# Graph attention on one core: the one-hots of the source numbers made at another place of the step, against numbers kept in PSUM

## The chip, the cores and the metric

The kernel runs on one core of a Trainium2 chip. The metric is the time of one execution in device microseconds. Five engines run their own instruction queues side by side: TensorE (PE, with its weight loads as PEld), VectorE (DVE), ScalarE (ACT), GpSimd (POOL) and SyncE (SP, which issues DMAs). They meet only through semaphores that one raises and another waits for.

## The reference

A graph has 3125 nodes of 128 features and 53125 edges, sorted by their target node `dst`. Two layers follow each other:

```
h = relu(layernorm(x))
Q, K, V = h @ Wq + bq, h @ Wk + bk, h @ Wv + bv          # 8 heads of 16
scores  = sum(Q[dst] * K[src]) * scale + edge_attr @ We + be
probs   = softmax of scores over the edges of one dst
x = x + segment_sum(probs * V[src], dst) @ Wo + bo
h = relu(layernorm(x));  h = logmap0(h) @ W.T + b
deg = in-degree + out-degree of each node, at least 1
x = x + expmap0(segment_sum(h[src] / sqrt(deg[src] * deg[dst]), dst))
```

The change touches only a side product of the first layer: the out-degrees, which are counts of each node number among the edges' sources `src`.

## The kernel before

A first stage makes Q, K and V for all nodes and writes them to tables in HBM. The attention loop then goes over the edges in 32 groups of 13 x 128 edges (`GROUPS`, `T`, `P`); a group's work on one engine is called its step here, and step g works on group g. Each engine has its own hand-written loop over the groups, whose order is the order of the code; two buffers of almost everything (index `b`) let an engine prepare group g + 1 during step g. The second layer comes after the loop.

What one step does, by engine:

- POOL gathers K and V rows of the next group into `kv` (13 indirect DMAs, line 812). It is held back to certain points of PE's step (`keep_step`).
- PE multiplies the target one-hots `ST` with a window of Q rows (`query`, line 1838, in four chunks of 4, 4, 4 and 1 tiles; chunks 0 and 1 of group g + 1 are done late in step g, chunks 2 and 3 early in step g + 1). Chunks share two PSUM buffers `ps_q`, so chunk 2 may start only when DVE has read chunk 0 out of the first (`s_prod`). PE also spreads row numbers (line 1825) that ACT turns into `ST` (lines 1608, 1610), sums the weighted rows of the group before (`window_sums`, line 1857), turns four small results around (`ps_b`: lines 1845, 1886, 1897, 1900), multiplies the two source one-hots into a histogram of source numbers (line 1892), and runs 16 matmuls whose result nobody reads (`stay_busy`, line 1815).
- DVE multiplies `kv` with `ps_q` (`product`, line 1080) and sums it by head (line 1086), chunk by chunk; adds the bias (line 1099); then four scans give a running maximum over the edges of one target, forward and backward within a partition (lines 1107, 1128) and over partitions (lines 1118, 1139), each with a PE turn between; then it weights the V rows (`weigh`, line 1164), prepares small matrices for the next step (lines 1135, 1026, 1030, 1156), and goes on to `product` of the next group.

The source one-hots: a source number is split into a high part (50 values) and a low part (64 values, `LO`), and `source_one_hots` (line 1050) compares the 13 parts of each partition with all 50 or 64 numbers, giving `oh_hi` (650 bf16 elements per partition) and `oh_lo` (832). The numbers to compare with lie in SBUF as `rep_hi`, in bf16, each number repeated 13 times. DVE's two instructions for group g + 1 stand in step g before and behind the first scan, where the scan waits for DVE's own bias add:

```
V.tensor_tensor(sc[:], sc[:], p_bias..., ALU.add).then_inc(s_sc, 1)
if more:
    source_one_hots(g + 1, 1 - b, (0,))
dve.wait_ge(s_sc, g + 1)
...                                     # the scan, raises s_v1
if more:
    source_one_hots(g + 1, 1 - b, (1,))
```

PE waits for them (`s_oh`) only before the histogram of group g + 1, a step later.

Of the kernel before, what the change touches and what calls it, by code (L numbers as in the profile page):

```python
# [23 lines left out]
ALU = mybir.AluOpType  # L24
# [3 lines left out]
P = 128  # L28
# [4 lines left out]
T = 13  # L33
# [12 lines left out]
HI, LO = 50, 64  # L46
# [98 lines left out]
def build(nc, x, src_t, dst_t, dst_before, dst_after, dst_first, dst_run, src_run, attr, wqkv, bqkv, we, be, wo, bo, w1t, b1,  # L145
# [14 lines left out]
    with ExitStack() as ctx:  # L160
        def sb(name, shape, dt=F32):
            return ctx.enter_context(nc.sbuf_tensor(name, shape, dt))

        def pb(name, shape, dt=F32):
            return ctx.enter_context(nc.psum_tensor(name, shape, dt))

        def sem(name):
            return ctx.enter_context(nc.semaphore(name))
# [3 lines left out]
        iota = sb("iota", [P, P])  # L172
# [42 lines left out]
        rep_hi = sb("rep_hi", [P, LO, T], BF16)  # L215
# [134 lines left out]
        ps_b = pb("ps_b", [P, 512])  # L350
# [7 lines left out]
        p_c2 = ps_b[:, 416:416 + H]  # L358
        p_rc = ps_c[:, 0:C + 1]
        p_fb = ps_c[:, 256:256 + H]  # L360

        s_in = sem("s_in")
        s_w = sem("s_w")
# [34 lines left out]
        s_oh = sem("s_oh")  # L398
# [131 lines left out]
        def known(g):  # L530

            return isinstance(g, int)
# [340 lines left out]
        def _(dve):  # L873
            V = nc.vector
            pre = Steps(nc, dve, s_dv0, 0)
# [10 lines left out]
            def set_idx(g, b, ready):  # L886

                V.tensor_copy(idx[:, b, :], src_i[:, g, :] if known(g) else
                              src_i[:, bass.ds(g, 1), :].rearrange("p g t -> p (g t)")).then_inc(ready, 1)
# [126 lines left out]
            def col(tile, g):  # L1016
                return tile[:, g:g + 1] if known(g) else tile[:, bass.ds(g, 1)]

            def col3(tile, g):
                return (tile[:, g:g + 1, :] if known(g) else tile[:, bass.ds(g, 1), :]).rearrange("p g t -> p (g t)")  # L1020

            def shift_matrix(g, b, used, ready):

                if not (known(g) and g < 2):
                    dve.wait_ge(used, g - 1)
                V.tensor_scalar(shift[:, b, :], imj[:], col(delta, g), None, ALU.is_equal).then_inc(ready, 1)
# [7 lines left out]
            edge_one_hots(0, 0, s_S, TA)  # L1034

            pre.mark(V.tensor_copy(iota_b[:], iota[:]))
            pre.mark(V.tensor_copy(rep_hi[:], iota[:, 0:LO].unsqueeze(2).to_broadcast([P, LO, T])))
            pre.then(V.tensor_scalar(part_i, src_i[:], 6, None, ALU.logical_shift_right))
            pre.then(V.tensor_copy(hi_f[:], part_i))
# [4 lines left out]
            def source_one_hots(g, b, parts=(0, 1)):  # L1044

                if 0 in parts and not (known(g) and g < 2):
                    dve.wait_ge(s_hist, g - 1)
                for i in parts:
                    oh, part, m = ((oh_hi, hi_f, HI), (oh_lo, lo_f, LO))[i]
                    V.tensor_tensor(oh[:, b], col3(part, g).unsqueeze(1).to_broadcast([P, m, T]),  # L1050
                                    rep_hi[:, 0:m, :], ALU.is_equal).then_inc(s_oh, 1)

            def add_counts(g):
                dve.wait_ge(s_hist, g + 1)
# [4 lines left out]
            def flat(tile):  # L1059
                return tile[:].rearrange("p h t -> p (h t)")  # L1060

            def reset8(tile, g):
                return (tile[:, g:g + 1] if known(g) else tile[:, bass.ds(g, 1)]).rearrange("p g h t -> p (g h t)")
# [7 lines left out]
            def scores(g, b, st, more, old):  # L1071

                def product(c):
                    t0, t1 = CH[c]
                    w = t1 - t0
                    dve.wait_ge(s_kv[b][c], 16 * w * ((g - b) // 2 + 1) if known(g) else (g + (2 - b)) * (8 * w))
                    dve.wait_ge(s_qt, NCH * g + c + 1)
                    if c >= 2:
                        st.sync()
                    V.tensor_tensor(prod[:, c % 2, 0:w, :], kv[:, b, t0:t1, 0:D],  # L1080
                                    ps_q[c % 2][:, 0:w * D].rearrange("p (t d) -> p t d", d=D), ALU.mult).then_inc(s_prod, 1)

                def per_head(c):
                    t0, t1 = CH[c]
                    dve.wait_ge(s_prod, NCH * g + c + 1)
                    st.mark(V.tensor_reduce(sc[:, :, t0:t1].rearrange("p h t -> p t h"),  # L1086
                                            prod[:, c % 2, 0:t1 - t0, :].rearrange("p t (h d) -> p t h d", d=DH),
                                            AX_X, ALU.add))

                product(0)  # L1090
                for c in range(NCH):
                    if c == OLD_ROWS:
                        settle(g, b, old)
                    if c + 1 < NCH:
                        product(c + 1)
                    per_head(c)
                st.sync()
                dve.wait_ge(s_bias, g + 1)
                V.tensor_tensor(sc[:], sc[:], p_bias.rearrange("p (t h) -> p h t", h=H), ALU.add).then_inc(s_sc, 1)
                if more:  # L1100
                    source_one_hots(g + 1, 1 - b, (0,))
                dve.wait_ge(s_sc, g + 1)

                if known(g) and g == 0:
                    dve.wait_ge(s_reset8, H)
                    dve.wait_ge(s_line, 16)
                V.tensor_tensor_scan(out=flat(f1), data0=reset8(fwd_reset8, g), data1=flat(sc), initial=BIG,
                                     op0=ALU.add, op1=ALU.max).then_inc(s_v1, 1)
                if more:
                    source_one_hots(g + 1, 1 - b, (1,))  # L1110

            def scan_partitions(g, b, st):

                dve.wait_ge(s_v1T, g + 1)
                if not (known(g) and g < 2):
                    dve.wait_ge(s_cfT, g - 1)
                st.mark(V.tensor_copy(c1[:, b, 0:1], c1[:, 1 - b, P:P + 1]))
                V.tensor_tensor_scan(out=c1[:, b, 1:P + 1], data0=lines(g), data1=p_v1, initial=c1[:, 1 - b, P:P + 1],
                                     op0=ALU.add, op1=ALU.max).then_inc(s_cf, 1)
# [47 lines left out]
            def carry(g, b, st):  # L1167

                dve.wait_ge(s_rc, g + 1)
                st.mark(V.tensor_scalar(fb[:], p_fb, 1.0, None, ALU.add))  # L1170
                st.mark(V.tensor_copy(R[:, b, C:C + 1], p_rc[:, C:C + 1]))
                st.sync()
                st.mark(V.tensor_tensor(R[:, b, 0:C].rearrange("p (h e) -> p h e", h=H),
                                        p_rc[:, 0:C].rearrange("p (h e) -> p h e", h=H),
                                        fb[:].unsqueeze(2).to_broadcast([P, H, DH + 1]), ALU.mult))

            def add_sums(g, b, st):

                st.sync()
                V.tensor_tensor(R[:, b, :], R[:, b, :], ps_r[:, 0:C + 1], ALU.add).then_inc(s_R, 1)  # L1180
# [27 lines left out]
            def settle(g, b, old):  # L1208

                if old:  # L1210
                    new_rows(g - 2, b)
                if not (known(g) and g == 0):
                    add_counts(g - 1)

            def step(g, b, edges=True, nodes=True, more=True, far=True, old=True):

                A = Steps(nc, dve, s_dA, NA * g)
                B = Steps(nc, dve, s_dB, NB * (g - 1))
                if edges:
                    scores(g, b, A, more, old)  # L1220
                else:
                    settle(g, b, old)
                if edges:
                    scan_partitions(g, b, A)
                if nodes:
                    carry(g - 1, 1 - b, B)
                if edges:
                    backward(g, b, A)
                if nodes:
                    add_sums(g - 1, 1 - b, B)  # L1230
                if edges:
                    if far:
                        set_idx(g + 2, b, s_idx)
                    scan_partitions_back(g, b, A)
                    shifted(g, b, A)
                if nodes:
                    average(g - 1, 1 - b, B)
                    B.check(NB)
                if edges:
                    weigh(g, b)  # L1240
                    first_row(g, A)
                    if more:
                        shift_matrix(g + 1, 1 - b, s_rc, s_S)
                        edge_one_hots(g + 1, 1 - b, s_S, TA)
                if edges:
                    factor(g)
                    A.check(NA)

            source_one_hots(0, 0)

            def tile_ids(k, st, idx_ready, rep_ready):
# [855 lines left out]
```

## Time and profile before

| | |
|---|---|
| median of 3 runs | 929.62 us (922.36 to 932.06) |
| profiled execution, its span | 938.0 us |
| PE busy | 824.9 us, 88% |
| DVE busy | 695.7 us, 74% |
| POOL busy | 588.5 us, 63% |
| ACT busy | 537.9 us, 57% |
| attention loop | about 46 to 625 us of the span |

The profile is of another execution than the three timed ones, and gives no time for itself beside its span; that span is 8.4 us above the median of the timed runs. Busy shares are means over the whole program. In a timeline a row is one or several equal instructions in a row: start, duration, engine, line, operation, output<-inputs, how many, and in brackets the idle time of the engine before it and what ended it. Starts of DVE instructions that wait for nothing lie a little before the end of the one ahead, since they overlap. Step 14 ends and step 15 begins at about 334 us; this pair of steps is the one that is read closely.

### The profile page before, as it was taken

Reading aid. Unit: us, or ns where it says so; the run is one execution under the profiler, and the core shown is the slowest. Engines: PE = TensorE matmul, PEld = TensorE weight load, DVE = VectorE, ACT = ScalarE, POOL = GpSimd, SP = SyncE. Lnnn points to the kernel's source line nnn. Section 1 sums busy time; section 2 is a strip of 40 time slices with the busy share of each in tenths; the row PEclk is TensorE's granted clock in tenths of the full one; section 3 lists DMA queues with packets and bytes.
Section 4 is the critical chain, followed back from the end, with each engine's and each line's share of the span. In section 5 each row is a group of like instructions: output and inputs, shape, how many; then the busy total and the mean of one; then the engine's idle time right before and its main releaser. Section 6 shows DMA issues by size and latency. Waiting matters only on the chain.

```text
span 938.0 us, 21433 instructions
## 1 busy us (share of the span) xinstructions
PE 824.9 (88%) x5435; PEld 625.1 (67%) x5435; DVE 695.7 (74%) x2543; ACT 537.9 (57%) x1360; POOL 588.5 (63%) x597
## 2 busy tenths in 40 slices
PE   5559988999999999999999999976599889989983
PEld 3236766767777777777677677764487677868673
DVE  8827745777777776787777777778988878888752
ACT  4486634566666666666665666607765455555530
POOL 0177755667777777777677777700466666666662
PEclk9868977999999999999999999997799999999997
DMA  6653445554544444444444444420422222222221
GB/s 175 208 137 90 115 105 95 113 126 117 128 123 118 136 113 119 131 117 120 128 113 126 128 115 133 120 77 19 107 58 60 65 53 70 56 67 59 64 60 28
DMA packets 103595, 95.99 MB, mean 102 GB/s; under 512 B 35964, under 2 KB 87393, under 8 KB 103553
## 3 DMA queue, kind: packets, MB, share of 16 engines
q0 software_dynamic: 25600, 66.10, 26.2%
q1 hardware_dynamic: 77961, 29.51, 12.7%
q8 instruction: 12, 0.20, 0.1%
q14 instruction: 22, 0.18, 0.1%
HBM read 84.40 MB, written 11.15 MB: 102 GB/s over the span
## 4 chain that ended last, share of the span: by engine, by line
PE 59%; POOL 14%; issue 9%; DMA 7%; DVE 5%; ACT 4%; SPq 2%; POOLq 0%; DVEq 0%
POOL kv L851 14%; PE ps_s L1815 13%; PE ps_q L1838 11%; PE ps_r L1857 10%; PE ps_f L1892 5%; DMA kv<-hs_tab,idx 4%; PE ps_c L1807 4%; PE ps_s L1825 4%; ACT ST L1608 3%; PE ps_f L1916 1%; PE ps_f L1915 1%; PE ps_c L1803 1%; PE ps_r L2017 1%; DMA qwin<-q_tab 1%; PE ps_c L1865 1%
## 5 line engine op out<-in xcount | busy, mean ns | idle before, releaser
L812 POOL DMA_INDIRECT kv<-kv_tab,idx x416 | 418.0, 1005 | 192.3 <-issue 125.3
L851 POOL DMA_INDIRECT kv<-hs_tab,idx x176 | 170.3, 967 | 141.0 <-DMA hs_tab<-qkv 54.4
L1608 ACT ACTIVATE ST<-ps_s,imj 128x512 f32<-128x512 f32 (+1 forms) x128 | 77.1, 602 | 150.1 <-PE ps_s L1825 150.0
L1815 PE MATMUL ps_s<-rep_hi,iota_b 128*128 128x512 bf16 x506 | 139.3, 393 | 0.0
L1838 PE MATMUL ps_q<-qwin,ST 128*128 128x128 f32 x832 | 128.6, 296 | 9.5 <-DMA qwin<-q_tab 6.0
L1838 PEld LDWEIGHTS ps_q<-qwin,ST 128*128 128x128 f32 x832 | 111.2, 201 | 24.8 <-issue 20.5
L1591 ACT ACTIVATE S<-iota,nloc 128x128 f32<-128x128 f32 x384 | 122.0, 389 | 0.0
L1080 DVE TENSOR_TENSOR prod<-kv,ps_q 128x512 f32<-128x512 f32 (+1 forms) x128 | 71.6, 575 | 62.7 <-PE ps_q L1838 60.4
L1857 PE MATMUL ps_r<-wv,S 128*128 128x137 f32 x832 | 111.1, 286 | 0.0
L1857 PEld LDWEIGHTS ps_r<-wv,S 128*128 128x128 f32 x832 | 103.4, 192 | 7.7 <-issue 6.8
L2017 PE MATMUL ps_r<-qkv,xt 128*128 128x128 f32 x800 | 92.0, 276 | 0.8 <-ACT xt L1733 0.8
L2017 PEld LDWEIGHTS ps_r<-qkv,xt 128*128 128x128 f32 x800 | 90.6, 192 | 1.1 <-issue 1.1
L1722 ACT ACTIVATE S<-iota,rest_nloc 128x128 f32<-128x128 f32 x176 | 56.3, 388 | 53.2 <-PE ps_f L2009 53.2
L1610 ACT ACTIVATE ST<-ST 128x512 f32<-128x512 f32 (+1 forms) x128 | 70.3, 550 | 4.0
L1815 PEld LDWEIGHTS ps_s<-rep_hi,iota_b 128*128 128x128 bf16 x506 | 42.3, 99 | 44.2 <-issue 15.4
L2028 PE MATMUL ps_f<-kv,S 128*128 128x128 f32 x352 | 46.9, 294 | 27.6 <-DMA kv<-hs_tab,idx 27.6
L1086 DVE TENSOR_REDUCE sc<-prod 128x32 f32<-128x512 f32 (+1 forms) x128 | 70.9, 574 | 0.0
L1825 PE MATMUL ps_s<-dloc_g,pick 32*128 32x512 bf16 (+1 forms) x128 | 44.9, 350 | 29.5 <-ACT ST L1608 22.4
L1487 DVE TENSOR_SCALAR ST<-bwd_reset 128x800 bf16<-128x800 f16 x128 | 56.3, 440 | 16.8 <-PE ps_q L2000 16.7
L2028 PEld LDWEIGHTS ps_f<-kv,S 128*128 128x128 f32 x352 | 44.4, 207 | 31.2 <-issue 20.4
L1164 DVE TENSOR_TENSOR wv<-kv,wv 128x1024 f32<-128x1024 f32 x64 | 62.5, 1019 | 0.5 <-ACT wv L1626 0.5
L1594 ACT ACTIVATE S<-S 128x512 f32<-128x512 f32 x96 | 60.5, 630 | 3.0
(278 smaller groups left out, 1382.1 us busy)
## 6 DMA issues: line engine op xcount, KB each, us to landing
kv<-kv_tab,idx POOLq DMA_INDIRECT x416, 2.8
attr_s<-in_attr SPq DMA_DIRECT2D x32, 192.0 KB
kv<-hs_tab,idx POOLq DMA_INDIRECT x176
kv_tab<-qkv SPq DMA_DIRECT2D x4, 640.0 KB, 3.4
x_tab<-x SPq DMA_DIRECT2D x32, 64.5 KB, 2.3
qwin<-q_tab SPq DMA_DIRECT2D x32, 64.0 KB
xwin<-in_x SPq DMA_DIRECT2D x32, 64.0 KB
xwin<-x_tab SPq DMA_DIRECT2D x32, 64.0 KB
```

The source lines that it names most:

```text
L812: pool.indirect_dma_start(out=kv[:, b, t, :], out_offset=None, in_=kv_tab, in_offset=bass.IndirectOffsetOnAxis(ap=idx[:, b, t:t + 1], axis ...
L851: pool.indirect_dma_start(out=kv[:, j, t, 0:D], out_offset=None, in_=hs_tab, in_offset=bass.IndirectOffsetOnAxis(ap=idx[:, j, t:t + 1], ax ...
L1080: V.tensor_tensor(prod[:, c % 2, 0:w, :], kv[:, b, t0:t1, 0:D], ps_q[c % 2][:, 0:w * D].rearrange("p (t d) -> p t d", d=D), ALU.mult).then ...
L1086: st.mark(V.tensor_reduce(sc[:, :, t0:t1].rearrange("p h t -> p t h"), prod[:, c % 2, 0:t1 - t0, :].rearrange("p t (h d) -> p t h d", d=DH ...
L1591: A.activation(S[:, b, t, :], iota[:], ACT.Abs, bias=nloc[:, g, t:t + 1] if known(g) else nloc[:, bass.ds(g, 1), t:t + 1].rearrange("p g t ...
L1608: A.activation(ST[:, b, t0:t1, :], row_index(c), ACT.Abs, bias=imj[:, 0:1], scale=-1.0).then_inc(s_sta, 1)
L1815: M.matmul(ps_s[1][:], iota_b[:], busy_cols, start=True, stop=True)
L1825: M.matmul(row_index(c), pick[:, b, :], dloc_g[:, t0:t1, :], start=True, stop=True)\
L1838: mm = M.matmul(ps_q[c % 2][:, (t - t0) * D:(t - t0 + 1) * D], ST[:, b, t, :], qwin[:, b, :], start=True, stop=True)
L1857: mm = M.matmul(ps_r[:, 0:C + 1], S[:, b, t, :], wv[:, t, :], start=(t == 0), stop=(t == T - 1))
L2017: M.matmul(sums[0], counts[:, i, :], hs_t[:, i, :], start=(i == 0), stop=False)
L2028: M.matmul(sums[1], S[:, j, t, :], kv[:, j, t, 0:D], start=(t == 0), stop=False)
```

## The change

Sixty-four fp32 numbers (0 to 63) are copied once into a free part of the PSUM bank `ps_b`. Both one-hot instructions of a group compare with these, each number read 13 times over, in place of `rep_hi`. And both move to the end of DVE's step, behind `weigh` and `first_row`, ahead of the preparation of the shift matrix. `rep_hi` stays, since `stay_busy` reads it.

```
+        p_iota = ps_b[:, 424:424 + LO]
...
+            pre.mark(V.tensor_copy(p_iota, iota[:, 0:LO]))
...
                     V.tensor_tensor(oh[:, b], col3(part, g).unsqueeze(1).to_broadcast([P, m, T]),
-                                    rep_hi[:, 0:m, :], ALU.is_equal).then_inc(s_oh, 1)
+                                    p_iota[:, 0:m].unsqueeze(2).to_broadcast([P, m, T]), ALU.is_equal).then_inc(s_oh, 1)
...
-                if more:
-                    source_one_hots(g + 1, 1 - b, (0,))
                 dve.wait_ge(s_sc, g + 1)
...
-                if more:
-                    source_one_hots(g + 1, 1 - b, (1,))
...
                     weigh(g, b)
                     first_row(g, A)
                     if more:
+                        source_one_hots(g + 1, 1 - b)
                         shift_matrix(g + 1, 1 - b, s_rc, s_S)
                         edge_one_hots(g + 1, 1 - b, s_S, TA)
```

DVE's queue around the bias add (`sc<-sc,ps_c`) and the first scan (`f<-fwd_reset,sc`), in the loop, before; a scan stands as SCALAR_TENSOR_TENSOR here, and ISA and REGISTER_ALU rows are the queue's own small instructions:

```order
L1099 TENSOR_TENSOR sc<-sc,ps_c 128x104
L1050 ISA
L1050 TENSOR_TENSOR oh_hi<-hi_f,rep_hi 128x650
L1107 ISA
L1107 SCALAR_TENSOR_TENSOR f<-fwd_reset,sc 128x104
L1050 REGISTER_ALU
L1050 TENSOR_TENSOR oh_lo<-lo_f,rep_hi 128x832
L1117 COPY c<-c 8x1
```

The same place of DVE's queue with the change:

```order
L1101 TENSOR_TENSOR sc<-sc,ps_c 128x104
L1107 ISA
L1107 SCALAR_TENSOR_TENSOR f<-fwd_reset,sc 128x104
L1115 COPY c<-c 8x1
L1116 ISA
```

The two one-hots are gone from here; the first scan follows the bias add at once.

DVE's queue at the end of the step, from the second half of the weighting to the first two products of the next group, before:

```order
L1164 TENSOR_TENSOR wv<-kv,wv 128x5x8x16
L1135 REGISTER_ALU
L1135 TENSOR_SCALAR isf<-iota,ofirst 8x128
L1026 ISA
L1026 TENSOR_SCALAR shift<-imj,delta 128x128
L1030 ISA
L1030 TENSOR_TENSOR S<-dloc,iota 128x128
L1156 SCALAR_TENSOR_TENSOR facd<-ident,fac 8x8
L1077 REGISTER_ALU
L1080 TENSOR_TENSOR prod<-kv,ps_q 128x512
```

The same place with the change:

```order
L1162 TENSOR_TENSOR wv<-kv,wv 128x5x8x16
L1133 REGISTER_ALU
L1133 TENSOR_SCALAR isf<-iota,ofirst 8x128
L1052 ISA
L1052 TENSOR_TENSOR oh_hi<-hi_f,ps_b 128x650
L1052 REGISTER_ALU
L1052 TENSOR_TENSOR oh_lo<-lo_f,ps_b 128x832
L1027 ISA
L1027 TENSOR_SCALAR shift<-imj,delta 128x128
L1031 ISA
L1031 TENSOR_TENSOR S<-dloc,iota 128x128
L1154 SCALAR_TENSOR_TENSOR facd<-ident,fac 8x8
```

Both one-hots, now with `ps_b` as an input, stand ahead of three small instructions and of the next group's first product.

## Rows read from the trace of the kernel before

**Rows 1.** By stretch: length; PE, PEld, DVE, ACT, POOL busy (count); PE clock; DMA.

```profile
200.00:400.00 200.00, 193.57 (x1249) 143.47 (x1249) 149.06 (x466) 126.96 (x314) 150.53 (x151) 0.99 0.47 123
369.00:372.40 3.40, 3.40 (x13) 2.33 (x12) 0.69 (x3) 1.32 (x2) 2.67 (x3) 0.50 0.40 116
```

**Rows 2.** One line of PE, 170 to 600 us: durations, first and last start.

```profile
L1900 PE MATMUL ps_b<-ident,c x25: 194/197/199, 174.2 to 588.6; 8*128 8x8 f32 x25
```

**Rows 3.** Who waited for whom, 170 to 600 us: total, times, longest.

```profile
DVE prod L1080 <- PE ps_q L1838: 32.8, 25, 2.7
```

**Rows 4.** Timeline of DVE around the first scan, step 14.

```profile
322.05 0.26 DVE L1099 TENSOR_TENSOR sc<-sc,ps_c 128x104 f32<-128x104 f32 x1
...
322.69 0.35 DVE L1107 TENSOR_TENSOR_SCAN f<-fwd_reset,sc 128x104 f32<-128x104 f32 x1
```

**Rows 5.** Timeline of PE at the same time.

```profile
320.55 2.85 PE L1857 MATMUL ps_r<-wv,S 128*128 128x137 f32 x22
323.23 0.27 PE L1845 MATMUL ps_b<-ident,f 128*8 128x128 f32 x1
```

**Rows 6.** Groups of DVE instructions by shape, 170 to 600 us: busy, mean ns.

```profile
L1080 DVE TENSOR_TENSOR prod<-kv,ps_q 128x512 f32<-128x512 f32 x75 | 48.8, 675 | 32.8 <-PE ps_q L1838 32.8
L1164 DVE TENSOR_TENSOR wv<-kv,wv 128x640 f32<-128x640 f32 x25 | 20.5, 819 | 0.0
L1050 DVE TENSOR_TENSOR oh_lo<-lo_f,rep_hi 128x832 bf16<-128x832 bf16 x25 | 14.9, 597 | 0.0
L1050 DVE TENSOR_TENSOR oh_hi<-hi_f,rep_hi 128x650 bf16<-128x650 bf16 x25 | 13.3, 533 | 0.0
...
L1080 DVE TENSOR_TENSOR prod<-kv,ps_q 128x128 f32<-128x128 f32 x25 | 6.8, 271 | 0.0
```

**Rows 7.** Timeline of DVE at the end of step 14.

```profile
332.61 0.27 DVE L1135 TENSOR_SCALAR isf<-iota,ofirst 8x128 f32<-8x128 f32 x1
332.80 0.27 DVE L1026 TENSOR_SCALAR shift<-imj,delta 128x128 f32<-128x128 f32 x1
...
333.34 0.67 DVE L1080 TENSOR_TENSOR prod<-kv,ps_q 128x512 f32<-128x512 f32 x1
```

**Rows 8.** Timeline of PE at the start of step 15.

```profile
334.63 0.82 PE L1815 MATMUL ps_s<-rep_hi,iota_b 128*128 128x512 bf16 x3
335.29 1.05 PE L1838 MATMUL ps_q<-qwin,ST 128*128 128x128 f32 x8
```

**Rows 9.** The same place at the start of step 1, DVE and PE.

```profile
78.97 0.67 DVE L1080 TENSOR_TENSOR prod<-kv,ps_q 128x512 f32<-128x512 f32 x1
...
79.79 1.13 PE L1838 MATMUL ps_q<-qwin,ST 128*128 128x128 f32 x8
```

**Rows 10.** The same place in step 31, DVE and PE.

```profile
610.68 0.69 DVE L1080 TENSOR_TENSOR prod<-kv,ps_q 128x512 f32<-128x512 f32 x1
...
611.58 0.29 PE L1838 MATMUL ps_q<-qwin,ST 128*128 128x128 f32 x1
```

**Rows 11.** The same place in step 4, DVE and PE.

```profile
129.97 0.69 DVE L1080 TENSOR_TENSOR prod<-kv,ps_q 128x512 f32<-128x512 f32 x1 [0.92 <-PE ps_q L1838]
...
138.62 0.63 PE L1838 MATMUL ps_q<-qwin,ST 128*128 128x128 f32 x2
```

**Rows 12.** Timelines of DVE and PE where the clock is low, step 17.

```profile
367.77 0.67 DVE L1080 TENSOR_TENSOR prod<-kv,ps_q 128x512 f32<-128x512 f32 x1
...
370.29 0.42 PE L1838 MATMUL ps_q<-qwin,ST 128*128 128x128 f32 x1
```

**Rows 13.** Timeline of DVE ahead of the loop's first product.

```profile
53.48 0.69 DVE L1080 TENSOR_TENSOR prod<-kv,ps_q 128x512 f32<-128x512 f32 x1 [6.35 <-PE ps_q L1838]
```

**Rows 14.** Timeline of POOL in step 14.

```profile
322.21 0.95 POOL L812 DMA_INDIRECT kv<-kv_tab,idx  x1 [0.31 <-issue]
...
329.18 0.94 POOL L812 DMA_INDIRECT kv<-kv_tab,idx  x1 [1.02 <-issue]
...
331.68 1.10 POOL L812 DMA_INDIRECT kv<-kv_tab,idx  x1 [0.30 <-issue]
```

More of the change, by code:

```diff
@@ L360, in build @@
         p_fb = ps_c[:, 256:256 + H]
+        p_iota = ps_b[:, 424:424 + LO]
         s_in = sem("s_in")
@@ L1036, in _ @@
             pre.mark(V.tensor_copy(iota_b[:], iota[:]))
+            pre.mark(V.tensor_copy(p_iota, iota[:, 0:LO]))
             pre.mark(V.tensor_copy(rep_hi[:], iota[:, 0:LO].unsqueeze(2).to_broadcast([P, LO, T])))
@@ L1050, in source_one_hots @@
                     V.tensor_tensor(oh[:, b], col3(part, g).unsqueeze(1).to_broadcast([P, m, T]),
-                                    rep_hi[:, 0:m, :], ALU.is_equal).then_inc(s_oh, 1)
+                                    p_iota[:, 0:m].unsqueeze(2).to_broadcast([P, m, T]), ALU.is_equal).then_inc(s_oh, 1)
             def add_counts(g):
@@ L1099, in scores @@
                 V.tensor_tensor(sc[:], sc[:], p_bias.rearrange("p (t h) -> p h t", h=H), ALU.add).then_inc(s_sc, 1)
-                if more:
-                    source_one_hots(g + 1, 1 - b, (0,))
                 dve.wait_ge(s_sc, g + 1)
@@ L1108, in scores @@
                                      op0=ALU.add, op1=ALU.max).then_inc(s_v1, 1)
-                if more:
-                    source_one_hots(g + 1, 1 - b, (1,))
             def scan_partitions(g, b, st):
@@ L1242, in step @@
                     if more:
+                        source_one_hots(g + 1, 1 - b)
                         shift_matrix(g + 1, 1 - b, s_rc, s_S)
```

## The prediction

> **What bounds the kernel now.** I read first the busy time by stretch, then the waits, then the timelines of one step on PE and DVE side by side. In the stretch from 200 to 400 us PE is busy 193.57 of 200 us, DVE 149.06, POOL 150.53 and ACT 126.96, and PE's clock is granted at 0.99 of 2.4 GHz [rows 1]. So PE sets the length of a step as long as nobody makes it wait. A line that PE runs once a step gives that length: its first and last of 25 starts lie 588.6 - 174.2 = 414.4 us apart over 24 steps, and with the 1.6 us of one slower step (below) taken off that is 17.20 us a step [rows 2].
>
> DVE waits in each of these steps. Before the third product it sits idle for the scores that PE makes, 32.8 us in 25 steps, or 1.31 us a step [rows 3]. That idle time is what the end of DVE's step may grow by before the *third* product is late. But the *first* product of the new group is wanted sooner: PE's query chunk 2 overwrites the buffer that the first product reads. In step 15 the first product ends at 333.34 + 0.67 = 334.01 [rows 7] and PE comes to chunk 2 at 335.29, straight from its three idle matmuls [rows 8]. The reader should see a gap of 1.28 us there, which no wait shows because PE doesn't wait yet.
>
> How much of the gap a semaphore takes is read from step 1, where PE already waits at this place: the first product ends at 78.97 + 0.67 = 79.64 and chunk 2 starts at 79.79, so 0.15 us passes from DVE's end to PE's start; and the eight matmuls that then start cold take 1.13 us [rows 9] where they take 1.05 us in step 15 [rows 8]. So the slack is 1.28 - 0.15 = 1.13 us, and once it is used up there is 0.08 us to pay on top.
>
> **The change part by part.**
>
> *The score part loses two instructions.* The bias add starts at 322.05 and takes 0.26, so the first scan could start at about 322.35 in place of 322.69 [rows 4], 0.34 us sooner. PE takes the scan's result at 323.23, in the midst of the window sums: 22 matmuls from 320.55 on, each 2.68 / 22 = 0.122 us after the other up to that turn [rows 5], with no idle time noted ahead of it. PE isn't waiting for this scan, so the 0.34 us only becomes DVE idle time ahead of the next scan. Gain: nothing. What hides that is PE's window sums; if they were shorter, the gain would be at most these 0.34 us a step.
>
> *The end of the step gains two dearer instructions.* No row shows a comparison of a bf16 part with fp32 numbers in PSUM. The nearest are the products, TENSOR_TENSOR with one fp32 input in PSUM: 675 ns for 512 elements and 271 for 128, so (675 - 271) / 384 = 1.052 ns an element [rows 6]. By these, oh_hi with 650 elements takes 271 + 522 x 1.052 = 820 ns and oh_lo with 832 takes 271 + 704 x 1.052 = 1012 ns. The bound below is what they take today with two bf16 inputs from SBUF, 533 and 597 ns [rows 6]; the bound above is the rate of the weighting with its 819 ns for 640 elements [rows 6], which gives 10 ns more each. I take the products, because the new instruction has their form: one fp32 operand in PSUM, one operand in SBUF. Starts follow each other 0.08 us before the end of the one ahead (332.61 + 0.27 against 332.80) [rows 7]. The insertion is thus 0.82 + 1.01 - 0.16 = 1.67 us; with today's durations it would be 0.97.
>
> In these rows a PSUM input costs no more at the start than an SBUF one: 675 - 512 x 1.052 = 136 ns for the product, 819 - 640 x 1.052 = 146 for the weighting, which reads SBUF alone [rows 6]. The Trainium skill says otherwise: "VectorE: DVE Perf Modes", section on the TRN2 errata, gives 58 fixed cycles for SBUF to SBUF and 120 for PSUM to SBUF at 0.96 GHz. By that page the two instructions would be an estimated 2 x 62 / 0.96 = 130 ns dearer together, and the sum below 26 x 0.13 = 3.4 us higher. The rows decide against it.
>
> *What stands behind the insertion.* On DVE that is the shift matrix, one tile of one-hots, the factor and then the first two products. The first three are wanted by PE only in the next step's window sums. The first product would end at 334.01 + 1.67 = 335.68, and chunk 2 could start at 335.68 + 0.15 = 335.83 in place of 335.29: 0.54 us later, and with the slower start of its matmuls 0.62 us. PE's queue is in order, so everything of PE behind it moves by as much: the spreading that ACT waits for, the window sums, the four turns. From the next turn of the backward scan DVE runs on PE's time again, and so the step is 0.62 us longer, 17.82 us. The third product's scores come 0.62 us later too, and DVE's idle time before it falls from 1.31 to 1.31 + 0.62 - 1.67 = 0.26 us.
>
> No DMA is issued by the moved step. SP waits for node rows that DVE makes behind the third product, and POOL for PE's turns, so both shift with PE. The histogram that reads the one-hots comes 10 us later, and the wait for the histogram before is long over.
>
> *In which steps.* Groups 1 to 31 have their one-hots made at the end of the step before. In step 1 PE already waits, so all 1.67 us counts. In step 31 the product ends at 611.37 and PE starts at 611.58 [rows 10]; 0.06 us is slack, so 1.6 us counts. In step 4 the product ends at 130.66 and PE comes only at 138.62, held up by the slow loads of Q rows [rows 11]; step 5 is alike; there the insertion is hidden. In step 17, where the clock is low, PE comes at 370.29 and the product ends at 368.44 [rows 12]: 1.85 - 0.15 = 1.70 us of slack, hidden. That leaves 26 steps at 0.62 us.
>
> *Before the loop* a copy of 64 numbers and the dearer first pair (0.7 us) stand ahead of a product before which DVE is idle for 6.35 us [rows 13]: nothing.
>
> **The sum:** 26 x 0.62 + 1.67 + 1.6 = 19.4 us more. The profiled execution's 938.0 us would be 957.4; it lies 8.4 us over the median of the three runs, so I put the sum on the median: 929.6 + 19.4 = 949.0 us.
>
> **The rivals.**
>
> *B, the one-hots stay as cheap as they are (not slower).* If DVE still makes two elements at a time, the insertion is 0.97 us, the first product ends at 334.98 and chunk 2 could start at 335.13, before PE comes at 335.29 [rows 7, 8]. Then 26 steps cost nothing, steps 1 and 31 about 0.95 each: 931.5 us. The point from which it turns is an insertion of 1.13 us. For it: today's pair runs at well under 1 ns an element [rows 6]. Against it: each instruction with an fp32 input in PSUM runs at 1.05.
>
> *C, faster.* The score part, and not PE's queue, would set the step: then the scan's 0.34 us comes off 31 steps, 929.6 - 10.5 = 919 us, if the insertion is hidden as in B. The even spacing of PE's matmuls up to the turn [rows 5] speaks against it. Another way to the same side is POOL. The gather beside the one-hots takes 0.95 us like the others, one beside the weighting 1.10, and at 329.18 POOL waits 1.02 - 0.30 = 0.72 us beyond its usual gap [rows 14]. So nothing is to be freed at the one-hots, and POOL doesn't set the pace. The Trainium skill, "SBUF — State Buffer", section on who interferes with whom, has a DVE instruction with two SBUF inputs contend with a GpSimd instruction that reads SBUF, which the one-hots would no longer do. By that rule two gathers a step would get up to 0.15 us shorter, as the weighting's are longer; with POOL as the pace that would be 31 x 0.3 = 9 us, about 920 as well. The trace shows the longer gather at the weighting and none at the one-hots.
>
> *D, slower by more: the clock.* The granted clock fell to 0.50 once in these steps, for 3.40 us [rows 1], which is worth at most 1.7 us of PE time. PE would now have some half a microsecond more idle time in each step, behind the idle matmuls. If the clock then falls in every fourth step, 7 times, it is 12 us more: 961 us. It decides from about five falls more than now.
>
> **How the numbers follow.** The forecast of 949 gets 0.72, D 0.11, B 0.10, C 0.05; 0.02 is left for what I don't see. The measurement can tell some 1% of this kernel, 9.3 us, from no change. The forecast and D are slower by over 1%, with a little of the forecast falling short (0.84 in all); B is within 1%, as is a forecast in which the insertion is only 1.3 us (0.12); C is faster (0.04). The forecast's own range is the sum with 0.45 to 0.75 us a step, 945 to 952, and the spread of the runs, -7 to +2.5 us, about it: 938 to 955. Upward the range takes in most of D, downward it stops short of B: 938 to 962.
>
> **What would show it.** In the profile after: oh_hi near 820 and oh_lo near 1010 ns; PE idle ahead of query chunk 2 with DVE's product as the releaser, about 0.5 us a step; DVE idle before the third product down to about 0.3 us; steps of 17.8 us; the gathers as long as before. I am wrong if the one-hots keep to 0.6 us, if PE doesn't wait at chunk 2, or if the clock row shows many falls.

## The result and the profile after

The changed kernel takes 945.7 us (median of 4, 944.72 to 952.82) against 928.15 us before (the three runs above and a fourth): the ratio is 1.0213 with a 95% interval of 1.0171 to 1.0256, or 16 to 24 us on 928. Runs of a slower state, over 1.5% above the fastest of their kernel, are left out of all ratios; that concerns three of the ten runs of one kernel below. The forecast was 949.0 us, or 19.4 us more.

The profiled execution after took 944.72 us with a span of 942.8, only 4.8 us over the span profiled before. The two spans don't compare, because of steps 4 and 5, in which the Q rows arrive late. PE waited for them 6.0 us in the kernel before and 2.8 us in the changed one, and before, the clock also fell behind these waits (0.86 from 100 to 160 us, against 1.00 after). From the first scan of step 3 to that of step 5 it took 49.42 us before and 36.95 after, 12.5 us less. In the profiles of the experiments this stretch takes 36.99 to 50.13 us, and 37.69 in one with the one-hots at their old place, so it doesn't go with the place; why it varies stays open.

The steady stretch of the changed kernel by busy time (length; PE, PEld, DVE, ACT, POOL; PE clock; DMA), which answers to [rows 1]:

```profile
200.00:400.00 200.00, 189.69 (x1212) 136.91 (x1210) 155.75 (x452) 123.35 (x305) 141.71 (x147) 1.00 0.44 119
```

In the steady stretch PE is now busy 189.69 of 200 us where it was 193.57, and DVE 155.75 where it was 149.06: PE waits more. How much a step grew is read from the line that PE runs once a step, here in the changed kernel from 173 to 600 us (first and last start):

```profile
L1899 PE MATMUL ps_b<-ident,c x24: 194/194/196, 184.1 to 593.7; 8*128 8x8 f32 x24
```

(593.7 - 184.1) / 23 = 17.81 us a step, where [rows 2] gave 17.20. The rest of this document compares kernels by this number, since it is free of what happens before the steady steps.

Where the 0.61 us go is seen at the end of DVE's step and in PE's queue beside it. DVE of the changed kernel, end of step 14:

```profile
330.35 0.81 DVE L1052 TENSOR_TENSOR oh_hi<-hi_f,ps_b 128x650 bf16<-128x650 f32 x1
331.09 1.00 DVE L1052 TENSOR_TENSOR oh_lo<-lo_f,ps_b 128x832 bf16<-128x832 f32 x1
332.02 0.27 DVE L1027 TENSOR_SCALAR shift<-imj,delta 128x128 f32<-128x128 f32 x1
...
332.56 0.67 DVE L1082 TENSOR_TENSOR prod<-kv,ps_q 128x512 f32<-128x512 f32 x1
```

and PE at the same time:

```profile
332.15 0.82 PE L1814 MATMUL ps_s<-rep_hi,iota_b 128*128 128x512 bf16 x3
333.38 0.35 PE L1837 MATMUL ps_q<-qwin,ST 128*128 128x128 f32 x1 [0.41 <-DVE prod L1082]
```

The one-hots stand where the shift matrix would start, at 330.35, and push it to 332.02. That is 1.67 us, to the second decimal what the prediction had. The first product ends at 332.56 + 0.67 = 333.23; PE has run its three idle matmuls and sits still until 333.38, with the product named as what it waited for. In [rows 7, 8] PE came to the same place 1.28 us after the product, without a wait. The waits of the changed kernel over 170 to 600 us (total, times, longest), which answer to [rows 3]:

```profile
DVE c L1115 <- PE ps_b L1844: 18.1, 24, 0.8
...
PE ps_q L1837 <- DVE prod L1082: 8.1, 23, 0.4
...
DVE prod L1082 <- PE ps_q L1837: 4.5, 24, 0.2
```

DVE's idle time before the third product is down from 1.31 us a step to 4.5 / 24 = 0.19, and a new idle time of 18.1 / 24 = 0.75 us stands behind the first scan: that is where the lighter score part went. The scan is sooner, and PE still turns it only when its window sums have come that far. The shift matrix and the tile of one-hots come later too, but the list has no wait of PE's matmuls for them: the first product is what PE waits for.

### The profile page after: what moved, and what is told of

Same layout as the page of the kernel before. It is cut to its first block, busy times and chain, and to the rows that moved or that the text cites. A ratio compares the mean times of both kernels' runs of the same rounds, so it can differ in the third digit from the quotient of the medians.

```text
span 942.8 us, 21434 instructions
## 1 busy us (share of the span) xinstructions
PE 822.0 (87%) x5435; PEld 614.9 (65%) x5435; DVE 722.0 (77%) x2544; ACT 538.2 (57%) x1360; POOL 573.9 (61%) x597
## 4 chain that ended last, share of the span: by engine, by line
PE 37%; DVE 23%; POOL 14%; issue 13%; DMA 6%; ACT 4%; SPq 2%; DVEq 1%; POOLq 0%
POOL kv L852 14%; PE ps_r L1856 10%; PE ps_s L1814 6%; PE ps_f L1891 5%; PE ps_q L1837 5%; DMA kv<-hs_tab,idx 4%; DVE oh_lo L1052 3%; PE ps_s L1824 3%; ACT ST L1607 2%; DVE wv L1162 2%; DVE oh_hi L1052 2%; DVE prod L1082 2%; PE ps_r L2016 1%; DMA qwin<-q_tab 1%; DVE c L1137 1%
## 5 line engine op out<-in xcount | busy, mean ns | idle before, releaser
L813 POOL DMA_INDIRECT kv<-kv_tab,idx x416 | 403.2, 969 | 211.1 <-issue 131.3
L1814 PE MATMUL ps_s<-rep_hi,iota_b 128*128 128x512 bf16 x506 | 137.0, 387 | 0.0
L1837 PEld LDWEIGHTS ps_q<-qwin,ST 128*128 128x128 f32 x832 | 105.2, 195 | 42.3 <-issue 29.8
```

Of the source, the lines that this page charges most:

```text
L813: pool.indirect_dma_start(out=kv[:, b, t, :], out_offset=None, in_=kv_tab, in_offset=bass.IndirectOffsetOnAxis(ap=idx[:, b, t:t + 1], axis ...
L1814: M.matmul(ps_s[1][:], iota_b[:], busy_cols, start=True, stop=True)
L1837: mm = M.matmul(ps_q[c % 2][:, (t - t0) * D:(t - t0 + 1) * D], ST[:, b, t, :], qwin[:, b, :], start=True, stop=True)
```

## The experiments

Three theories. **Threshold**: only PE's wait at query chunk 2 lengthens the step, so an insertion at the end of DVE's step is free up to 1.13 us and counts one for one beyond. **Proportional**: DVE's longer step counts in its share wherever it lies. **PSUM**: reading the numbers from PSUM disturbs, not the place. In each batch the kernel before ran on the same chip: 926.09 us (19 runs) for place only, PSUM only, behind the first product and no idle matmuls, and 934.26 us (13 runs) for the other four, which fell on a slower chip. The change itself is compared with the 928.15 us of the section above. Step lengths can be compared across the batches: the change with 1.67 us inserted has 17.81 us a step, and 1.68 us, on the slower chip, give 17.82.

The insertion is by how much the time from the end of the weighting to the first product grew, and the length of a step is read as above from the line that PE runs once a step. The idle matmuls are those of `stay_busy`, whose result nobody reads.

| kernel | insertion, us | us a step | ratio to before, 95% interval |
|---|---|---|---|
| before | 0 | 17.20 | 1 |
| place only | 0.95 | 17.21 | 1.0033, 1.0010 to 1.0056 |
| low part from PSUM | 1.36 | 17.53 | 1.0159, 1.0074 to 1.0244 |
| the change | 1.67 | 17.81 | 1.0213, 1.0171 to 1.0256 |
| bf16 read 13 times | 1.68 | 17.82 | 1.0215, 1.0131 to 1.0300 |
| PSUM only | 0 | 17.33 | 1.0040, 1.0021 to 1.0059 |
| behind the first product | 0 | 17.29 | 1.0069, 1.0042 to 1.0095 |
| bf16 behind the first product | 0 | 17.23 | 1.0003, 0.9958 to 1.0047 |
| no idle matmuls | 1.67 | 20.53 | 1.1108, 1.1083 to 1.1133 |
| idle matmuls moved | 0 | 16.80 | 0.9854, 0.9788 to 0.9921 |

**The place alone.**

```
-                                    p_iota[:, 0:m].unsqueeze(2).to_broadcast([P, m, T]), ALU.is_equal)
+                                    rep_hi[:, 0:m, :], ALU.is_equal)
```

> The one-hots stand at the end of the step, but compare with the bf16 numbers in SBUF as before. Theory 'threshold' (PE's query chunk 2 waits for the first product, and the insertion costs only what exceeds 1.13 us): the insertion is about 0.97 us, PE's step stays at 17.20 us, only steps 1 and 31 lose about 1 us each: about 930 us, within 2 us of before. Theory 'proportional' (whatever DVE does more at the end of the step lengthens it in its share; 1.67 us cost 0.61): 0.97 us cost 0.35 us a step, 11 us in all, about 939 us. Theory 'PSUM' (the reading of PSUM disturbs, not the place): also no change.

Measured 929.12 us beside 926.09, 17.21 us a step. The line that PE runs once a step, and DVE and PE of this kernel at the start of a step:

```profile
L1898 PE MATMUL ps_b<-ident,c x24: 194/194/198, 180.1 to 576.0; 8*128 8x8 f32 x24
...
323.27 0.67 DVE L1081 TENSOR_TENSOR prod<-kv,ps_q 128x512 f32<-128x512 f32 x1
...
324.24 0.27 PE L1836 MATMUL ps_q<-qwin,ST 128*128 128x128 f32 x1
```

The product ends at 323.94 and PE comes at 324.24, with no idle time noted: 0.30 us are left of the 1.28, and 0.15 of these the semaphore takes. 0.95 us more of DVE at the end of the step cost the steady steps 0.01 us. "Proportional" (939 us) falls; "PSUM" forecast the same as "threshold" here and isn't tested. The 3 us that stay are of the size of steps 1 and 31, where nearly no slack was left: the first scans of steps 0 and 1 lie 1.33 us further apart than before, those of steps 30 and 31 1.25 us.

**The operand alone**, at the old place, in a bank that PE leaves alone at that time:

```
+        p_iota = ps_f[:, 448:448 + LO]
...
-                                    rep_hi[:, 0:m, :], ALU.is_equal)
+                                    p_iota[:, 0:m].unsqueeze(2).to_broadcast([P, m, T]), ALU.is_equal)
```

> The one-hots stand around the first scan as before, but compare with fp32 numbers in PSUM (in a bank that PE leaves alone at that time). The instructions should take 0.81 and 1.00 us as in the changed kernel. Theory 'threshold': the first scan ends about 0.28 us later, PE's turn of it, which has some 0.04 us to spare after the semaphore, waits about 0.24 us a step, 7 us in all: about 936 us, and the gap at chunk 2 stays near 1.3 us. Theory 'PSUM' (the operand costs wherever it is read): 17 us as in the changed kernel. Theory 'place' (the operand is harmless): no change.

Measured 929.3 us beside 926.09, 17.33 us a step: 0.13 us more, half of what was expected. The first scan and PE's turn of it:

```profile
311.75 0.37 DVE L1110 TENSOR_TENSOR_SCAN f<-fwd_reset,sc 128x104 f32<-128x104 f32 x1
...
312.18 0.28 PE L1848 MATMUL ps_b<-ident,f 128*8 128x128 f32 x1
```

The scan ends at 312.12 and PE follows after 0.06 us, so the semaphore took less here than the 0.15 us I had taken. The operand costs something at the old place too, but a fifth of the change's 0.61 us: "PSUM" falls as the main cause.

**The same two instructions behind the first product.**

```
                 product(0)
+                if not (known(g) and g == 0):
+                    source_one_hots(g, b)
...
-                        source_one_hots(g + 1, 1 - b)
```

> The two instructions of the changed kernel, with PSUM operand and all, stand behind the first product of their own group in place of ahead of it. DVE's work is the same. Theory 'threshold': the first product ends in time again, the second product ends at 336.3 on the clock of step 15 where PE wants it at 336.6, the third is 0.4 us late, and the scan gets 0.34 us of that back: steps of 17.2 to 17.3 us, 929 to 933 us. Theories 'proportional' and 'PSUM' (DVE's added work or the operand itself): about 946 us as in the changed kernel.

Measured 932.83 us beside 926.09, and 17.29 us a step. DVE does the same work from the same PSUM numbers as in the changed kernel, one product later, and 0.52 of the 0.61 us a step are gone. So it is what stands behind the insertion that costs. The total is 7 us over before, at the upper end of what was expected; 26 x 0.09 us make 2.3 of them. Of the rest, the trace shows 1.66 us between the first scans of steps 0 and 1 and 1.39 between those of steps 30 and 31; steps 4 and 5, with their late Q rows, leave the remainder open.

**An insertion between the two.**

```
+                    numbers = rep_hi[:, 0:m, :] if i == 0 else p_iota[:, 0:m].unsqueeze(2).to_broadcast([P, m, T])
...
-                                    p_iota[:, 0:m].unsqueeze(2).to_broadcast([P, m, T]), ALU.is_equal)
+                                    numbers, ALU.is_equal)
```

> As the changed kernel, but only the low part compares with the PSUM numbers; the high part takes the bf16 numbers from SBUF. The insertion at the end of the step is then 0.45 + 0.92 = 1.37 us, between the 0.95 of the place alone (17.20 us a step) and the 1.67 of the changed kernel (17.80). Theory 'threshold' (slack 1.13 us, then one for one, and 0.08 us for a cold start of the matmuls): 0.24 + 0.08 = 0.32 us a step, steps of 17.5 us, with 1.3 us each in steps 1 and 31 some 11 us in all: about 937 us. Theory 'proportional': 0.50 us a step, about 942 us.

Measured 948.24 us beside 934.26, 17.53 us a step:

```profile
L1900 PE MATMUL ps_b<-ident,c x24: 194/196/199, 186.3 to 589.6; 8*128 8x8 f32 x24
```

That is 0.33 us more, where "threshold" gave 0.32 and "proportional" 0.50. The total (ratio 1.0074 to 1.0244) is too wide to tell the two apart; the step length does. With 0.95, 1.36 and 1.67 us inserted the step grows by 0.01, 0.33 and 0.61 us: flat at 0.95, and from 1.36 to 1.67 nearly one for one (0.28 us for 0.31). The point from which it counts lies between 0.95 and 1.36.

**What makes the instructions dear.**

```
-                                    p_iota[:, 0:m].unsqueeze(2).to_broadcast([P, m, T]), ALU.is_equal)
+                                    iota_b[:, 0:m].unsqueeze(2).to_broadcast([P, m, T]), ALU.is_equal)
```

> As the changed kernel, but the 64 numbers lie in SBUF in bf16, each read 13 times over (step 0), in place of fp32 in PSUM. It tells what makes the two instructions dear. Theory 'PSUM or fp32': with three bf16 operands they take 0.53 and 0.60 us again, steps of 17.20 us, about 929 us as with the place alone. Theory 'step 0': an operand whose elements don't lie side by side is as dear as PSUM, 0.81 and 1.00 us, steps of 17.8 us, about 945 us.

Measured 953.68 us beside 934.26, 17.82 us a step. The two instructions here, and below them those of the changed kernel (both from the view of one line: duration least/median/most):

```profile
L1051 DVE TENSOR_TENSOR oh_hi<-hi_f,iota_b x32: 764/817/819, 46.2 to 617.4; 128x650 bf16<-128x650 bf16 x32
L1051 DVE TENSOR_TENSOR oh_lo<-lo_f,iota_b x32: 1003/1006/1008, 46.9 to 618.2; 128x832 bf16<-128x832 bf16 x32
```

```profile
L1052 DVE TENSOR_TENSOR oh_hi<-hi_f,ps_b x32: 811/812/831, 46.5 to 615.1; 128x650 bf16<-128x650 f32 x26, 128x650 bf16<-128x650 bf16 x6
L1052 DVE TENSOR_TENSOR oh_lo<-lo_f,ps_b x32: 1000/1001/1011, 47.3 to 615.9; 128x832 bf16<-128x832 f32 x26, 128x832 bf16<-128x832 bf16 x6
```

With three bf16 operands in SBUF they are as dear as with fp32 in PSUM, once one of them reads each element 13 times over. "PSUM or fp32" falls as the only reason: the repeated read is enough by itself. Whether a PSUM operand without the repeated read would be, no run tells. And since no PSUM is read here at 17.82 us a step, it wasn't the bank `ps_b` either, which PE writes too. The Trainium skill, "VectorE: DVE Perf Modes", section on mode 2x_1P, asks for 16-bit values and steps of plus or minus one for two elements a cycle. The trace agrees that the repeated read costs: with it the 182 elements between the two instructions take 189 ns, 1.04 ns each, and with the numbers stored repeated 64 ns [rows 6].

**Cheap one-hots at the free place.** The bf16 numbers of the first experiment at the place of the third.

> The bf16 numbers in SBUF, and the one-hots behind the first product of their own group, where DVE is idle for 1.3 us a step ahead of the third product; the insertion is 0.95 us. Theory 'threshold': nobody waits for it, steps of 17.20 us, the lead of the first product over chunk 2 back at 1.25 us, and steps 1 and 31 lose nothing: about 926 us, as before. If DVE's freer score part were worth something, it would be a few us faster than before.

Measured 936.13 us (median of seven runs; 938.81 of all ten) beside 934.26, a ratio of 1.0003 (0.9958 to 1.0047), and 17.23 us a step. In the steady steps nobody waits for them there, and the freer score part is worth nothing. That is "threshold", and with the place alone it settles that the steady steps had nothing to gain by taking the one-hots out of the score part. That step 31 loses nothing was missed: the first scans of steps 30 and 31 lie 1.22 us further apart than before.

**The changed kernel without the idle matmuls** ahead of chunk 2:

```
-BUSY = (3, 4, 3, 3, 3)
+BUSY = (0, 4, 3, 3, 3)
```

> The changed kernel without the three idle matmuls ahead of query chunk 2 (0.65 us of PE a step). Theory 'threshold': PE waits there for DVE's first product, so it only waits 0.65 us longer: steps stay at 17.8 us and the time at 946 us within 2 us, unless the granted clock falls for the longer idle time, which the clock row would show. Theory that PE's own work still sets the step: 0.65 us less a step, about 926 us.

Measured 1028.91 us beside 926.09, 20.53 us a step. The time didn't stay, because the clock fell in the steps. A stretch of this kernel by busy time, PE at its start, and the wait over 180 to 590 us:

```profile
350.20:357.00 6.80, 6.75 (x26) 5.36 (x26) 4.20 (x12) 2.75 (x5) 4.02 (x5) 0.50 0.41 103
...
349.97 0.41 PE L1837 MATMUL ps_q<-qwin,ST 128*128 128x128 f32 x1 [1.04 <-DVE prod L1082]
...
PE ps_q L1837 <- DVE prod L1082: 22.2, 20, 1.2
```

After 1.04 us of idle time the granted clock is 0.50 (1.2 GHz) for 6.8 us, and 1.00 for the 13.7 us after it; from 190 to 600 us, 20 such steps, its mean is 0.83, as these two stretches give. So the time can't decide between the two theories: half the clock for 6.8 us costs an estimated 3.4 us of PE, and less the 0.65 us taken out that would be 2.75, beside 2.72 measured. What decides is the wait. PE now idles 22.2 / 20 = 1.11 us ahead of chunk 2 where it idled 0.35, about the 0.65 us more that "threshold" expects. In this kernel the idle matmuls thus hold the clock up even where PE waits anyway.

**The idle matmuls moved**, in the kernel before:

```
                 if edges:
-                    stay_busy(BUSY[0])
+                    stay_busy(1)
                     query(g, b, (2,))
...
                     query(g, b, (3,))
+                if edges:
+                    stay_busy(2)
                 if edges and more:
                     spread_rows(g + 1, 1 - b, (2,))
```

> The kernel before, with two of the three idle matmuls ahead of query chunk 2 moved behind chunk 3, where PE waits 0.36 us a step for ScalarE. By the theory that PE's queue sets the step of the kernel before, and waits there only at that place: chunk 2 comes 0.43 us sooner, the wait is filled, steps of about 16.85 us, 11 us faster, about 915 us, if the granted clock stays up; chunk 2's lead falls to about 0.8 us. If something else sets the step (gathers, VectorE's chain): no change, about 926 us.

Measured 922.64 us (922.06 to 922.75) beside 934.26, a ratio of 0.9854 (0.9788 to 0.9921), 16.80 us a step: faster than both kernels. The wait for ScalarE in the kernel before (170 to 600 us), and the line that PE runs once a step in this one:

```profile
PE ps_s L1825 <- ACT ST L1608: 9.0, 25, 0.4
...
L1902 PE MATMUL ps_b<-ident,c x24: 194/194/199, 186.3 to 572.6; 8*128 8x8 f32 x24
```

Two of the idle matmuls now run where PE waited 9.0 / 25 = 0.36 us for ScalarE's row numbers; this wait stands no longer in the list of this kernel, and the step is 0.40 us shorter. This also shows that PE's queue set the step of the kernel before, which the prediction took as its first step.

## Why the prediction was right

**What bounds the kernel**: right. The moved idle matmuls shorten the step by about the wait that they fill, and freeing DVE's score part gains nothing.

**The price of the two instructions**: right in size, 812 and 1001 ns against 820 and 1012, and lucky in its reason. It was read from instructions with an fp32 operand in PSUM, and I gave that form as the reason; the read of each number 13 times over does it alone. The number came out because both kinds run at one element in about 1.05 ns. By the same reasoning bf16 numbers in SBUF would have been priced at today's 533 and 597 ns, read 13 times over or not. The dearer start from PSUM that the Trainium skill gives ("VectorE: DVE Perf Modes", section on the TRN2 errata) shows in no row: 812 and 1001 from PSUM stand beside 817 and 1006 from SBUF.

**The slack at chunk 2 and its semaphore**: right. 1.67 inserted cost 0.61 a step against 0.62, and the point from which it counts lies between 0.95 and 1.36 us, as 1.13 does. In the step shown PE starts 0.15 us after the product's end (333.23 to 333.38), as in step 1 before. The idle time noted there is shorter than the 0.5 us forecast (8.1 / 23 = 0.35) because the three idle matmuls are noted as longer than they hold up PE: in [rows 8] they take 0.82 us, and chunk 2 starts 0.66 us after them. With these 0.16 us the wait is 0.51.

**The steps**: right for the steady ones and step 31, not shown for step 1. The steady steps give 26 x 0.61 = 15.9 us, and step 31 shows its share. DVE and PE of the changed kernel there, as in [rows 10]:

```profile
618.09 0.69 DVE L1082 TENSOR_TENSOR prod<-kv,ps_q 128x512 f32<-128x512 f32 x1
...
618.93 0.35 PE L1837 MATMUL ps_q<-qwin,ST 128*128 128x128 f32 x1 [1.43 <-DVE prod L1082]
```

PE waits 1.43 us there. In step 1 it waits 1.13 us and the clock then falls (0.63 from 84.0 to 88.5 us), so that the first scans of steps 0 and 2 lie 4.16 us further apart than before; less step 2's own 0.6 that is some 3.5 us where the prediction put 1.67. In "bf16 read 13 times", with the same insertion, it is 1.0. With the prediction's 1.6 and 1.67 the sum is 19.2 us. The medians differ by 17.6, and the interval of the ratio holds both. Steps 4 and 5 vary by up to 13 us from profile to profile, so the last 2 us aren't shown either way.

**The rivals**: B fell by the durations, C by the two kernels that leave the score part free without a gain (17.21 us a step with the place alone, 17.23 with the bf16 one-hots behind the first product). POOL's gathers beside the moved one-hots take what others take, and the long one stands at the weighting again (changed kernel, POOL):

```profile
329.23 1.09 POOL L813 DMA_INDIRECT kv<-kv_tab,idx  x1 [0.30 <-issue]
330.63 0.95 POOL L813 DMA_INDIRECT kv<-kv_tab,idx  x1 [0.30 <-issue]
```

D didn't happen in the steady steps of the changed kernel, whose clock is granted in full from 100 to 600 us; the kernel without idle matmuls shows how near it was, 0.65 us of PE away.

## What to carry to other kernels

A wait that costs nothing yet has a length: find for each instruction that is moved who waits for what stands behind it, and subtract. Up to that slack a move is free, beyond it each microsecond counts in every step. Work taken off an engine at a place where nobody waits for it gains nothing, however busy the engine is. And matmuls that only keep TensorE busy cost less where it waits anyway: here 0.40 us a step less, with the clock still granted in full in the steady steps.

## What the runs showed of the hardware that was not expected

A TENSOR_TENSOR with three bf16 operands in SBUF takes 817 ns for 650 elements if one operand reads each of its elements 13 times over, and about 0.53 us if the same numbers lie there repeated [rows 6]. And TensorE's clock, which stayed up in steps with a wait of 0.4 us, fell to half when idle matmuls were taken out and that wait grew to 1.04 us. The length of one wait doesn't decide it: behind the 1.43 us of step 31 in the changed kernel the clock stayed at 1.00 (600 to 640 us), and behind the 1.13 us of its step 1 it fell.
